# Expert items: token lists by one-hot products, rows gathered raw and normalised per item, items ordered by batch, batch 0 prepared beside the last items

## The reference, cut to what matters

```python
x = x + tanh(g_xattn) * experts(layernorm(x), token_ids)
x = x + tanh(g_ffn) * ffn(layernorm(x), ...)

# experts: 4 experts, chosen by the token's id; W[e] (512 x 512) is gate, up and down at once
out = zeros
for e in range(4):
    g = silu(h @ W[e].T); u = h @ W[e].T; y = (g * u) @ W[e].T
    out = where(expert_of(token) == e, y, out)

# ffn: attention of 16 heads of 32, its output used only through a product with A (rank 16)
attn = attention(rmsnorm(x) * ln1)
mod = 0.1 * tanh(attn @ A)
h = rmsnorm(x) * ln2
out = x + (silu(h @ Win.T + mod * (h @ A) @ B) * (h @ Wup.T)) @ Wdown.T
```

## Time and profile before

| | us |
|---|---|
| median of 3 runs (1155.48 to 1157.55) | 1156.31 |
| the profiled execution | 1155.6 |
| its span in the profile | 1153.6 |
| first product of item 0 starts | 52.5 |
| last product of the items ends | 180.3 |
| batch 0's first projection starts | 209.3 |
| batch 1's first projection starts | 447.9 |

### The profile page before, as it was taken

One profiled execution on the slowest core, in us unless ns is written; L12 is line 12 of the kernel. 1 busy time (PEld: TensorE's weight loads), 2 busy tenths in 40 slices (PEclk: granted clock), 3 DMA queues, 4 the chain that ended last, 5 costly groups with the idle time before them and its releaser, 6 DMA issues.

```text
span 1153.6 us, 18580 instructions
## 1 busy us (share of the span) xinstructions
PE 1053.0 (91%) x5384; PEld 885.5 (77%) x5385; DVE 719.8 (62%) x1591; ACT 622.8 (54%) x1466; POOL 167.4 (15%) x138
## 2 busy tenths in 40 slices
PE   0299995899999999998999999989999999899998
PEld 0178885688778888887788888877888888778887
DVE  7332326589766555898565558995564589944443
ACT  4233331588654444786544437885444378854442
POOL 4520002123300000333000013230000033200000
PEclk9999996799999999999999999999999999999999
DMA  7555231533333332523432326324332353323331
GB/s 276 189 141 163 92 109 56 169 69 82 120 110 93 98 118 84 137 55 100 138 99 82 121 65 167 68 65 163 93 98 82 100 157 81 73 73 92 93 98 45
DMA packets 52977, 124.44 MB, mean 108 GB/s; under 512 B 7441, under 2 KB 7441, under 8 KB 52369
## 3 DMA queue, kind: packets, MB, share of 16 engines
q1 hardware_dynamic: 50368, 115.55, 34.1%
q0 software_dynamic: 2560, 8.39, 2.1%
HBM read 80.92 MB, written 17.83 MB: 86 GB/s over the span
## 4 chain that ended last, share of the span: by engine, by line
PE 76%; DVE 11%; issue 5%; ACT 5%; DMA 2%; POOL 1%; DVEq 0%; ACTq 0%; SPq 0%; POOLq 0%
PE bank L479 60%; PE bank L629 5%; PE bank L642 4%; PE bank L611 3%; DVE wr L1177 3%; DVE nb L1189 3%; ACT big L881 2%; PE bank L671 1%; ACT wr L793 1%; DVE big L1198 1%; PE bank L613 1%; ACT big L805 1%; DVE wch L1227 1%; POOL x_sorted L404 1%; PE bank L501 1%
## 5 line engine op out<-in xcount | busy, mean ns | idle before, releaser
L479 PE MATMUL bank<-wr,wch 128*128 128x512 f32 x1536 | 373.2, 392 | 0.0
L479 PEld LDWEIGHTS bank<-wr,wch 128*128 128x128 f32 x1536 | 288.0, 188 | 64.0 <-issue 1.2
L479 PE MATMUL bank<-wch,actr 128*128 128x512 f32 x768 | 185.5, 391 | 3.6 <-DVE actr L1177 3.6
L479 PEld LDWEIGHTS bank<-wch,actr 128*128 128x128 f32 x768 | 143.4, 188 | 35.0 <-DVE actr L1177 5.3
L1227 DVE SCALAR_TENSOR_TENSOR wch<-stream,lns,wch 128x256 fp32r<-128x256 f32 x256 | 122.3, 539 | 50.9 <-ACT wch L920 50.9
L1177 DVE TENSOR_TENSOR wr<-bank,wr 128x512 fp32r<-128x512 f32 (+1 forms) x240 | 135.0, 608 | 29.2 <-ACT wr L793 28.8
L881 ACT ACTIVATE big<-bank,nb 128x512 f32<-128x512 f32 (+3 forms) x256 | 131.5, 531 | 15.9 <-DVE nb L1189 14.8
L793 ACT ACTIVATE wr<-bank 128x512 fp32r<-128x512 f32 (+1 forms) x240 | 111.3, 535 | 37.8 <-PE bank L479 22.8
L793 ACT ACTIVATE actr<-act_sb 128x512 fp32r<-128x512 f32 x64 | 40.4, 632 | 147.3 <-DVE act_sb L1240 147.3
L479 PE MATMUL bank<-wr,actr 128*128 x456 | 116.6, 406 | 3.3 <-DVE actr L1142 1.5
L1189 DVE TENSOR_REDUCE nb<-bank 128x1 f32<-128x512 f32 (+3 forms) x256 | 107.2, 479 | 6.5 <-PE bank L613 5.9
(11 more groups left out here) (152 smaller groups left out, 1162.5 us busy)
## 6 DMA issues: line engine op xcount, KB each, us to landing
stream<-in_wmlp SPq DMA_DIRECT2D x64, 512.0 KB, 4.0
stack<-wr SPq DMA_DIRECT2D x192, 128.0 KB, 2.3
stream<-in_wmlp SPq DMA_DIRECT2D x64, 256.0 KB, 2.7
big<-in_x SPq DMA_DIRECT2D x8, 1024.0 KB, 7.9
xi<-x_sorted SPq DMA_DIRECT2D x19, 256.0 KB, 2.6
y_sorted<-ysb SPq DMA_DIRECT2D x19, 256.0 KB, 2.0
stream<-in_wexp SPq DMA_DIRECT2D x4, 1024.0 KB, 11.2
residual<-big SPq DMA_DIRECT2D x4, 1024.0 KB, 5.2
```

The source lines that it names most:

```text
L479: mm = pe.matmul(dst, lhs(pl, k), rhs(pr, k), start=start and i == 0, stop=stop and i == n - 1, skip_group_check=skip)
```

## The change

- SP loads the experts into four places of their own (two in `stream`, two in `wstage`), with Wo and Wv (into the memory of tiles 0 to 7 of `big`) and batch 0's x between them; Wq and Wk come in one load when the experts are split. x is not loaded for the items.
- VectorE works out for each token its item (items now ordered by batch: those of batch 0's tokens first) and its place in the item. One-hot blocks of place and item are multiplied on TensorE, which gives for each item the list of its 128 rows and its weight offset: `gidx` to gather, `sidx` to scatter (rows of no token go to a row past the end), `itab` for the weights.
- GpSimd gathers raw rows of x per item into a ring of eight tiles and scatters each item's y to its tokens' rows (`y_rows`), a gather ten items ahead. `item_stats` and `item_factors` (by groups of 1, 3, 3, 4, 4, 4 items) are on VectorE, `normalise_rows` on ScalarE, within the item loop. GpSimd also makes the low part of expert 0, the split of B (high part) and the scaling of Wq and Wk between the scatters.
- `Wo @ A` and `Wv` by it stand ahead of the items. Batch 0's x1, factors, normalised rows, turns and splits stand beside items 10 to 18. `hT` and `wqs` have memory of their own; `wch` lies in that of `wr`.
- Later batches' y is loaded by SP in one piece (`load_y`) in place of GpSimd's four gathers.

The loops over items on VectorE and ScalarE are written out item by item.

```diff
+RING = (12, 13, 14, 15, 0, 1, 2, 3)
+GROUPS = ((0,), (1, 2, 3), (4, 5, 6), (7, 8, 9, 10), (11, 12, 13, 14), (15, 16, 17, 18))
...
 # SP
+            load_expert(0)
+            sp.dma_start(araw[:, :, :], amat).then_inc(a_in, 16)
+            sp.dma_start(wo_raw, wov[:, 0, :]).then_inc(wo_in, 16)
+            load_expert(1)
...
+            load_expert(2)
+            sp.dma_start(wv_raw, wov[:, 1, :]).then_inc(wv_in, 16)
+            load_expert(3)
+            sp.dma_start(x1, x_tiles[0]).then_inc(x1_in, 16)
+            sp.wait_ge(exp_hi, E)
+            sp.wait_ge(exp_lo, E)
+            sp.dma_start(wstage[:, :, :], wqk).then_inc(wqk_in, 16)
...
             sp.wait_ge(vw_mm, 2)
+            sp.wait_ge(y_stored, 16 * FIRST_ITEMS)
+            sp.dma_start(hb, y_tiles[0]).then_inc(y_in, 16)
+            sp.wait_ge(bst_ok, 3)
+            for c in range(2):
+                load_chunk(0, c, c, first=True)
             store_residual(0)
...
+            sp.wait_ge(y_stored, 16 * ITEMS)
             batch(0, True, first=True)
...
 # GpSimd
+            pool.wait_ge(exp_hi, 1)
+            g.tensor_tensor(wr[:, LO, 0:EW], expert_raw(0), wr[:, HI, 0:EW].bitcast(F32), ALU.subtract)
...
+            def turn(i):
+                for k in range(NS + 2 if i else NS, NS + 3):
+                    if i + k < ITEMS:
+                        gather(i + k)
+                scatter(i)
+            pool.wait_ge(index_ok, 1)
+            for i in range(NS):
+                gather(i)
...
+            for k in range(4):
+                g.tensor_copy(bst[:, cols], braw[:, cols]).then_inc(bst_hi, 1)
+                turn(k + 1)
+            pool.wait_ge(wqk_in, 16)
+            for dt in range(DT):
+                turn(5 + dt)
+                g.tensor_scalar(wqk_v[:, 0, dt, :], wqk_v[:, 0, dt, :], lns[:, 0, dt:dt + 1], SCALE, ...)
+                ins = g.tensor_scalar(wqk_v[:, 1, dt, :], wqk_v[:, 1, dt, :], lns[:, 0, dt:dt + 1], ...)
...
 # TensorE
+            for t in range(NT):
+                pe.wait_ge(place_ok, t // (NT // OC_PARTS) + 1)
+                mm = pe.matmul(bank[0][:, 128:128 + 2 * IC], inv_lhs[:, t, :],
+                               inv_rhs[:, t, :, :].rearrange("p m i -> p (m i)"), start=t == 0, stop=t == NT - 1)
...
             def turn_x(i, first=False):
-                pe.wait_ge(xi_in, i * 16 + 16)
+                pe.wait_ge(xn_ok, i + 1)
...
+            with pe.Fori(2, last - 2) as i:
+                item_step(i)
+            for i in (last - 2, last - 1):
+                item_step(i)
...
+                for dt in (0, 1) if i == last - 2 else (2, 3):
+                    turn_rows(0, (dt,), FIRST_ROWS)
...
             def batch(b, more):
                 pe.wait_ge(ht_lo, b * 4 + 4)
-                for which in range(2):
-                    project(b, 0, which, FIRST_QK[which])
+                project(b, 0, 0, FIRST_QK[0])
+                pe.wait_ge(y_copied, ITEMS)
+                project(b, 0, 1, FIRST_QK[1])
...
 # ScalarE
+            for i in range(1, ITEMS - 1):
+                silu(i)
+                x_high(i + 1)
+                if i + 2 < ITEMS:
+                    normalise_rows(i + 2)
+                if i == ITEMS - 2:
+                    rows_high(0, (0, 1), FIRST_ROWS)
+                copy_y(i - 1)
+                act_high(i)
...
 # VectorE
+            v.tensor_scalar(gidx[:, :], bank[0][:, 128:128 + IC], own_row, float(T - 1), ...).then_inc(index_ok, 1)
...
+            expert_low(1)
+            expert_low(2)
+            item_stats(0)
+            item_factors(0)
+            expert_low(3)
+            for i in GROUPS[1]:
+                item_stats(i)
+            x_low(0)
+            item_factors(1)
+            gated(0)
...
+            for i in range(1, ITEMS - 1):
+                gated(i)
+                x_low(i + 1)
+                if i == 1:
+                    item_stats(6)
+                    item_factors(2)
+                elif i in (2, 3):
+                    item_stats(2 * i + 3)
+                    item_stats(2 * i + 4)
+                elif i == 4:
+                    item_factors(3)
...
+                elif i == 8:
+                    item_factors(4)
...
+                elif i == 12:
+                    x1_tile(0, 2)
+                elif i in (13, 14):
+                    norm_factors(0, i - 13)
+                act_low(i)
+                if i == 3:
+                    values_low()
+                elif i in (6, 7):
+                    low_rank_low(i - 6)
+                elif i in (10, 11, 12):
+                    x1_tile(0, (0, 1, 3)[i - 10])
+                elif i in (15, 16):
+                    residual(0, 2 * (i - 15))
+                    residual(0, 2 * (i - 15) + 1)
+                elif i == ITEMS - 2:
+                    rows_low(0, (0, 1), FIRST_ROWS)
```

More of the change, by code:

```diff
@@ L39 @@
 ROWS = (0, 3, 6, 7)
+FIRST_ROWS = (0, 1, 2, 3)
 FIRST_QK = (6, 7)
@@ L335, in batch @@
             def batch(b, more, first=False):
-                if first:
-                    for c in range(2):
-                        load_chunk(b, c, c, first=True)
                 for j in range(2):
@@ new lines, in _ @@
+            expert_high(0)
+            expert_high(1)
+            act.wait_ge(bd_zero, 1)
+            act.wait_ge(woa_ok, 1)
+            woa = bank[1][:, 0:DT * R].rearrange("p (c r) -> p c r", c=DT)
+            for h in range(QH):
+                rows = slice(HD * h, HD * h + HD)
+                ins = copy(bd[rows, :, h, :], woa[rows, :, :])
+            ins.then_inc(bd_ok, 1)
+            act.wait_ge(small_in, 32)
+            a.activation(tg[:, :], gt[:, :], ACT.Tanh).then_inc(tanh_ok, 1)
@@ L1388, in _ @@
-            ins.then_inc(prep_ok, 1)
-            for j in range(TT):
-                residual(0, j)
-            rows_low(0)
+            expert_low(1)
[8 more added lines that the diff above has]
+            gated(0)
+            x_low(1)
+            item_stats(4)
+            item_stats(5)
+            act_low(0)
```

613 lines of the change are left out of this document (321 added, 292 removed).

## The result

The changed kernel takes **1114.76 us** (median of 4 runs, 1114.36 to 1115.36) against 1155.89 us for the kernel before in the same session (4 runs, 1154.34 to 1157.55): ratio **0.9644, 95% interval 0.9628 to 0.9661**. Forecast were 1110.5 us, in a range of 1103 to 1122. The direction and most of the mechanism held; the gain is 41.1 us, 4.4 less than the 45.5 forecast, and some of what is missing lies in places that the prediction had put at zero. The time also lies 0.8 us above the narrower 1106 to 1114 that the prediction gave to its own case.

What follows compares the result with a forecast made beforehand. TensorE was taken to bound items and batches, leaving some 84 us open in prologue, bridge and batch 0's start. Terms -29.0 - 2.8 + 2.1 - 17.3 + 1.5 = -45.5 us gave 1110.5 us, range 1103 to 1122.

Steps and rivals of the forecast that it cites:

- The bridge: Stretch between items and batch 0: its work moves ahead of or beside the items, minus 29.0 us.
- the seam: Last item to batch 0: second projection and stack loads stay hidden, zero; sixteen transposes between products add 2.1 us.
- Batch 0: First batch after the items: starts at full clock and costs what batch 1 costs, minus 2.8 us.
- later batches, zero: Batches after batch 0: loading y by SP in one piece instead of four gathers costs nothing.
- The prologue: Stretch before the first product: first product at 35.2 us instead of 52.5, minus 17.3 us.
- GpSimd's first gather, issued at 20.3, should have landed by then: Prologue: gather 0's rows land at 25.0 us, before VectorE ends two low parts at 25.4.
- The items: Item loop: stalls from work laid into it, plus 1.5 us; sixteen transposes between products, plus 2.1 us.
- collision at item 8: Item loop: VectorE's factors start within a GpSimd scaling and may stand for 1.8 us, plus 1.2 us.
- The port cost more than one stall: Rival, item loop: three items lose 2.2 us each and a late scatter 1.5; 1118.5 us, chance 0.15.
- GpSimd never set the period: Rival, item loop: GpSimd's queue of gathers and scatters sets the item period, slower than before, 1163.7 us; chance 0.03.
- The prologue is later: Rival, prologue: slower index steps and gathers behind full queues, first product at 43, 1118.5 us; chance 0.12.
- the quick prologue: Rival, prologue: no collision in the index chain and a warm first product, 1105.5 us; chance 0.10.

Runs made afterwards that it cites:

- e7: Changed kernel with batch 0's 16 turns and the splits of hT moved back behind the last item; 1117.86 us, ratio 0.9693 to the kernel before.
- e5: Changed kernel with expert 0's low part moved from GpSimd to VectorE, it and expert 1's ahead of the index list's last step; 1108.90 us, ratio 0.9613.
- e1: Changed kernel with VectorE held from the low parts of experts 1 and 2 until GpSimd has issued gather 0; 1114.74 us, ratio 0.9652.
- e6: Changed kernel with the edits of e5 and e1 together: low parts early on VectorE, and the hold for gather 0; 1111.11 us, ratio 0.9635.
- e2: Changed kernel with a one-column silu on ScalarE ahead of item 0's rows, so silu's table loads early; 1112.43 us, ratio 0.9636.
- e11: Changed kernel with GpSimd's three memsets moved behind gathers 8 to 10; 1110.63 us, ratio 0.9629.
- e4: Changed kernel with the loads of batch 0's first two chunks waiting for 10 and 12 stored items instead of 7; 1112.96 us, ratio 0.9641.
- e3: Changed kernel with 16 filler matmuls on TensorE between the Wv products and item 0's turn; 1115.36 us, ratio 0.9666.
- e10: Changed kernel with e4's later chunk loads and GpSimd's third and fourth pair of scalings moved from behind scatter 7; 1112.63 us, ratio 0.9648.

## Why the prediction was right, and where it was short

**The bridge and the seam: right.** Minus 29.0, projections at full speed right behind the last product, turns at 1.7 us (forecast 2.1). e7 shows that the turns are worth having inside: outside, the wait and the clock cost more than they save.

**Batch 0: the size came near for a reason that needs correcting.** The cold start was worth 8.45 - 5.60 = 2.85 us, as forecast. Against it stand 0.74 us of a late load into `stack`. The term "later batches, zero" failed by the same wait, 0.73 us in batches 1 and 2 as well. Over all, stack loads land 2.3 us after issue (median), in the kernel before at most 2.4 in the stretch of this wait, in the kernel after up to 3.1. Batch 1's minus 0.9 is this wait and a stretch at a lower clock (1.55 us, at 460.77 before) that it no longer has; that was luck, since nothing ties such a stretch to the edit. Why these loads land later was not tried; no experiment changed how they or y are loaded.

**The prologue: right in mechanism, short by 3.1 us.** The step that failed is "GpSimd's first gather, issued at 20.3, should have landed by then". The prediction had the rule at hand (the issue of the earlier trace rows that took 2.60 us and ended 0.8 us after a subtraction) and used it for the index chain, but not for the gather, which it laid beside two subtractions. With one of them, at the 5.8 us that e5 took from the issue's start to the rows, they would have come at about 26.1 (an estimate); it was held through both, which no row had shown, and they came at 29.77. e1, e5 and e6 give 1.17, 3.30 and 1.17 us for none, one and none beside it, against 5.51. From the rows to the first product it was 8.6 us, forecast 9.8: the 0.8 us set aside there for gather issues among the small steps was not needed. The list itself was 1.3 us late: the prediction let the inversion products end 0.9 us behind the last one-hot block, because TensorE would only wait for its left sides. They took 3.57 us, the upper end of the 1.8 to 3.6 given for them, and ended 1.9 us behind it, at 21.2. The loads' line is a little off in itself (its rows give 3.0 us for each MB, the times go up by 2.9), which bounds nothing here.
The Trainium skill (SBUF — State Buffer, SBUF: two separate sides) says that GpSimd cannot write descriptors while VectorE runs an operation in a mode that also takes the port pair the two share, such as a copy in fp32, and that the DMA is then blocked until VectorE's end plus some 115 ns. The trace agrees on the block, though here it was a subtraction with both inputs in SBUF that held an indirect DMA. By the page's figure and the issues' own lengths (1.17 us for gather 0, 0.95 for later ones) an estimate has them end 1.29 and 1.07 us after VectorE's end; measured were 1.05 and 1.06 for gather 0 in e5 and after, and 0.83, 0.83 and 0.82 for three later issues in e1, some 0.24 us less in both.

**The items: 4.7 us against 3.6, by other things than named.** The start-up is 2.5 us longer (11.3 to 13.7), which no step of the prediction held: a table load that the old order had hidden, a step held by a memset, and a second product at a lower clock. e2 and e11 show it. The "collision at item 8" (1.2 us) was there, but in the kernel after it caught two small steps, 1.0 us in all, and cost TensorE nothing; where it caught three, in e4 and e1, it cost 0.9. What stands in its place in after is the late scatter (0.7). For the scatter the prediction had counted only GpSimd's queue; its landing beside 2.5 MB of loads was not in the sum. The scalings took 0.71 to 1.73 us and 1.57 to 1.59 us, not 2.2. With the turns at 1.7 instead of 2.1, the sum came to 4.7.

**The rivals.** The port cost more than one stall (gather 0, the three-column step), but in the prologue and the start of the items, not in three items of the loop; GpSimd never set the period. A scatter was late, as this rival had it, but by the loads and not by the port (e4). "The prologue is later" came half true, for the port and not for full queues. The mechanism of the quick prologue (no collision, warm first product) was made in e5 and e3: the first gave 3.9 us at batch 0, the second 0.4 at the third product.

## What to carry to other kernels

When work moves ahead of a loop, list for every DMA that GpSimd issues there which VectorE operations with two SBUF inputs run beside it, and put them before or behind the first issue on which all depends. Look for what a new order lays open: a table load, a memset, a burst of loads in front of a small store. A wait can cost more than its length, if the product behind it then runs at a lower clock (2.6 us for a table load of 1.28). Two stalls in one place can cover each other, so judge a cure by the start of the next stage and not by the stall that it removes.

## What the runs showed of the hardware

- Gather 0's issue, begun 0.02 us after a VectorE subtraction, ended 1.05 us (e5) and 1.06 us (after) behind the last of those that followed each other (5.51 us with two, 3.30 with one, 1.17 with none). But the second issue of e1, begun 0.13 us after a subtraction at 23.33, ended at 26.45, 0.83 us behind the first and in the middle of the next one (25.54 to 27.82). When an issue slips in between two and when not stays open.
- A GpSimd memset of 96x2048 (1.83 us) held a VectorE step on 128x3 for 1.88 us; moved away, the step took 0.35. Where GpSimd's scalings of 128x512 came, two or three steps on four columns took 0.62 to 0.75 us (after, e4), without them 0.16 (e10).
- A scatter of 128 rows landed 7.5 us after its issue behind 2.5 MB of queued loads, 3.4 at most without 1.5 MB of them (e4); the median is 2.7.
- The first product took 5.48 us in a stretch for which the profile gives a granted clock of 1.00 (38.36 to 43.90); with TensorE busy from 27.93 to 34.10 ahead of it (e3), it took 3.03. In six profiles with the same prologue (after, c_after, e4, e7, e10, e11) it took 4.33 to 5.48. Here the duration shows the half rate and the clock's column does not.
